# Two of each expert's eight second products in rounded form, and a new order around the last layer's transposes

## What is computed

```python
x = x + xattn_0(layernorm(x), ctx, ...)          # softmax of a normalised similarity
x = x + moe(layernorm(x), ...)                   # 8 experts and a shared one, low-rank side path
x = x + xattn_1(ctx, ctx, masks, layernorm(x))   # masked softmax, scores scaled by the normalised x
x = x + lut_ffn(layernorm(x), lut, gate_idx, up_idx, down_idx)

# moe: top 2 of 8 experts for 1024 tokens, 160 tokens for each expert and choice
h = gelu(einsum('ecd,edf->ecf', buf, w1) + b1[:, None, :])      # 256 -> 1024
y = einsum('ecf,efd->ecd', h, w2) + b2[:, None, :]              # 1024 -> 256
y = y + einsum('ecr,erd->ecd', gelu(einsum('ecd,edr->ecr', buf, wd)), wu)
# lut_ffn: weights are looked up, w = lut[idx], 256 -> 688 -> 256
h = silu(x @ gate.T) * (x @ up.T);  out = h @ down.T
```

## Time and profile before

| | |
|---|---|
| median of 3 runs | 305.8 us (305.75 to 312.18) |
| profiled execution | 306.0 us |
| its span | 304.2 us |
| TensorE busy | 290.8 us, 96% |
| VectorE busy | 240.4 us, 79% |
| ScalarE busy | 155.3 us, 51% |
| POOL busy | 116.5 us, 38% |
| TensorE clock granted | full in all of the span |

### The profile page before, as it was taken

How to read it: one execution, slowest core, us unless ns; L and a number is a source line. 1 busy time by engine, 2 the same in 40 slices (tenths; PEclk the granted TensorE clock), 3 DMA queues, 4 the chain that set the end, 5 groups by cost and what they waited for, 6 DMA issues and landing times.

```text
span 304.2 us, 5858 instructions
## 1 busy us (share of the span) xinstructions
PE 290.8 (96%) x1911; PEld 253.1 (83%) x1911; DVE 240.4 (79%) x638; ACT 155.3 (51%) x369; POOL 116.5 (38%) x143
## 2 busy tenths in 40 slices
PE   7988998998999999999999999999999999989895
PEld 5545686977888998989989898999888899979795
DVE  4888878638989888889888898898985768796632
ACT  2677986225554755546556465555533633535210
POOL 7427410150518165280743806042061224443431
PEclk9999999999999999999999999999999999999999
DMA  7933207540958539195482935647044000010101
GB/s 214 328 139 95 80 0 230 171 138 5 296 163 221 172 79 349 52 253 174 101 286 61 291 134 131 209 78 226 1 43 140 0 1 2 0 37 0 37 0 69
DMA packets 21841, 38.06 MB, mean 125 GB/s; under 512 B 3131, under 2 KB 12411, under 8 KB 21820
## 3 DMA queue, kind: packets, MB, share of 16 engines
q1 hardware_dynamic: 17340, 32.55, 32.5%
q0 software_dynamic: 4480, 5.25, 9.2%
HBM read 31.37 MB, written 6.42 MB: 124 GB/s over the span
## 4 chain that ended last, share of the span: by engine, by line
PE 74%; DVE 12%; ACT 7%; issue 2%; POOL 2%; DMA 1%; SPq 0%; DVEq 0%; ACTq 0%
PE yb L799 27%; PE hb L780 27%; PE yb L814 6%; PE hb L925 4%; PE tb L692 4%; PE yb L940 1%; POOL rstd L454 1%; PE rb L940 1%; DVE xn L1195 1%; PE yb L925 1%; DMA projw<-projw_dram 1%; ACT sm L982 1%; DVE bst L1189 1%; DVE h L1667 1%; DVE x L1338 1%
## 5 line engine op out<-in xcount | busy, mean ns | idle before, releaser
L799 PE MATMUL yb<-raw,h 128*128 128x256 f32 x384 | 96.3, 380 | 0.1
L1095 ACT ACTIVATE h<-hb,b 128x320 f32<-128x320 f32 (+1 forms) x80 | 44.5, 558 | 63.7 <-PE hb L780 59.0
L799 PEld LDWEIGHTS yb<-raw,h 128*128 128x128 f32 x384 | 69.0, 189 | 7.4 <-ACT h L1095 0.5
L780 PE MATMUL hb<-xT_hi,w_hi 128*128 128x320 f32 (+1 forms) x180 | 71.4, 397 | 0.5 <-ACT small L1099 0.5
L780 PE MATMUL hb<-xT_lo,w_hi 128*128 128x320 f32 (+1 forms) x180 | 58.7, 326 | 0.0
L780 PE MATMUL hb<-xT_hi,w_lo 128*128 128x320 f32 (+1 forms) x180 | 58.6, 325 | 0.0
L554 POOL DMA_INDIRECT xacc_dram<-ysb,row_of x16 | 28.5, 1778 | 77.8 <-ACT ysb L962 75.4
L1221 DVE COPY_PREDICATED pick<-bits,pick 128x544 int32<-128x544 uint8 x56 | 43.3, 774 | 0.6
L538 POOL DMA_INDIRECT xg<-xnorm_dram,row_of x24 | 28.7, 1197 | 34.4 <-DVE row_of L1479 17.8
L1580 DVE TENSOR_TENSOR w_lo<-raw,w_hi 128x256 fp32r<-128x256 f32 x84 | 34.7, 415 | 7.4 <-ACT w_hi L962 7.3
L780 PEld LDWEIGHTS hb<-xT_hi,w_hi 128*128 128x128 f32 x180 | 33.9, 188 | 5.1 <-issue 2.2
(11 more groups left out here) (226 smaller groups left out, 512.5 us busy)
## 6 DMA issues: line engine op xcount, KB each, us to landing
raw<-w1pack_dram SPq DMA_DIRECT2D x30, 384.0 KB, 4.9
raw<-w2pack_dram SPq DMA_DIRECT2D x30, 384.0 KB
idx<-idx_dram SPq DMA_DIRECT2D x8, 272.0 KB
x<-x_dram SPq DMA_DIRECT2D x4, 256.0 KB, 4.7
xnorm_dram<-xn SPq DMA_DIRECT2D x2, 512.0 KB, 5.8
xacc_dram<-x SPq DMA_DIRECT2D x2, 512.0 KB, 8.4
x<-xacc_dram SPq DMA_DIRECT2D x4, 256.0 KB, 3.9
out_dram<-x SPq DMA_DIRECT2D x4, 256.0 KB, 2.1
```

What stands on the lines that cost most here:

```text
L780: mm = pe.matmul(hb[s % RING][:, 0:n], w[:, s, k * P:(k + 1) * P], a[:, turn, k, 0:n], start=(i == 0), stop=(i == len(terms) - 1))
L799: mm = pe.matmul(yb[c // 2][:, (c % 2) * D:(c % 2 + 1) * D], h, w, start=(s == 0 and c % 2 == 0), stop=(s == STEPS - 1), skip_group_check= ...
L1095: act.activation(hidden(s - 1, shared, turn), bank[:, 0:n], ACT.Gelu, bias=b1[:, expert, s - 1:s])\
```

## The change

It has three parts. In experts, steps 3 and 5 of the second product are no longer fp32. ScalarE copies w2's eighth and the GELU's rows, 256 columns each, into parts of `h_hi`, VectorE subtracts both into `h_lo`, and TensorE runs three fp32r products of the parts for each of the two blocks: six matmuls for two. The third block stays as it was. `h_hi` and `h_lo` are the last layer's buffers, idle until then. In unit 1 `low_rows` also moves ahead of the first two lookup slots.

In the last layer the transposes of batches 2 and 3 move behind the last gate group of the batch before, and the down product that stood behind the next batch's first group moves ahead of it; `finish` moves from group 3 to group 4, behind the split of the transposes. The last batch's second tile gets a bank of its own (`tb[0]`), and its two tiles are added and sent out one by one.

```diff
+ROUNDED = (3, 5)
...
+            for i in range(2):
+                sp.wait_ge(x4_ok, B + i)
+                sp.dma_start(t["out"][B - 1, i * P:(i + 1) * P, :], x[:, 2 * B - 2 + i, :]).then_inc(out_done, 16)
+            sp.wait_ge(out_done, 16 * B + 16)
...
+            def second_rounded(u, s, loads):
+                i = ROUNDED.index(s)
+                pe.wait_ge(pair_lo_ok, u * 4 + 2 * i - 2)
+                for c in range(2):
+                    rows = slice(c * P, (c + 1) * P)
+                    for j, (h, w) in enumerate(((h_hi, h_hi), (h_lo, h_hi), (h_hi, h_lo))):
+                        mm = pe.matmul(yb[0][:, c * D:(c + 1) * D], h[:, 2 + i, rows], w[:, i, :],
+                                       start=False, stop=False, skip_group_check=True)
+                mm.then_inc(mm2, 1)
...
+                    elif s - LAG in ROUNDED and not shared:
+                        second_rounded(u, s - LAG, loads)
...
+                        apart = b == B - 1 and i == 1
+                        out = tb[0][:, 0:D] if apart else down_banks[b % 2][:, i * D:(i + 1) * D]
...
-                if n >= GLAG:
+                if n == 2 * NG - 1 or n == 3 * NG - 1:
+                    transpose_x3(n // NG + 1)
                     down((n - GLAG) // NG, (n - GLAG) % NG)
-                if n % NG == 4 and n // NG + 1 < B:
-                    transpose_x3(n // NG + 1)
+                    down((n - GLAG + 1) // NG, (n - GLAG + 1) % NG)
+                elif n >= GLAG and n != 2 * NG and n != 3 * NG:
+                    down((n - GLAG) // NG, (n - GLAG) % NG)
+                if n == NG - 2:
+                    transpose_x3(1)
...
+            def pair_weights_hi(u, turn, i):
+                s = ROUNDED[i]
+                act.wait_ge(raw2_in[turn][s // 3], (u - turn) * 8 + 16)
+                act.wait_ge(mm2, u * STEPS - STEPS + s + 1)
+                copy(h_hi[:, i, :], raw2[:, turn, s, :]).then_inc(pair_hi_ok, 1)
+            def pair_rows_hi(u, turn, i):
+                s = ROUNDED[i]
+                act.wait_ge(h32_ok, u * NF + s)
+                copy(h_hi[:, 2 + i, :], hidden(s - 1, False, turn)[:, 0:S]).then_inc(pair_hi_ok, 1)
...
+            def pair_lo(u, turn, i):
+                s = ROUNDED[i]
+                dve.wait_ge(pair_hi_ok, u * 4 + 2 * i - 3)
+                dve.wait_ge(mm2, u * STEPS - STEPS + s + 1)
+                dve.tensor_tensor(h_lo[:, i, :], raw2[:, turn, s, :], h_hi[:, i, :].bitcast(F32), ALU.subtract)\
+                    .then_inc(pair_lo_ok, 1)
+                dve.wait_ge(pair_hi_ok, u * 4 + 2 * i - 2)
+                dve.tensor_tensor(h_lo[:, 2 + i, :], hidden(s - 1, False, turn)[:, 0:S], h_hi[:, 2 + i, :].bitcast(F32),
+                                  ALU.subtract).then_inc(pair_lo_ok, 1)
...
-                    if s == 1 and u:
+                    if s == 1 and u and not after_shared:
                         low_rows(u, UTOK if shared else SLOTS)
...
+                    if s == 0 and after_shared:
+                        low_rows(u, SLOTS)
...
+                if f == 4 and b > 0:
+                    finish(b - 1)
...
-                if f == 3 and b > 0:
-                    finish(b - 1)
-            finish(B - 1)
+            last = 2 * B - 2
+            dve.wait_ge(last_tile_mm, 1)
+            dve.tensor_tensor(x[:, last, :], x[:, last, :], down_banks[(B - 1) % 2][:, 0:D], ALU.add).then_inc(x4_ok, 1)
+            dve.wait_ge(down_mm, B * NG)
+            dve.tensor_tensor(x[:, last + 1, :], x[:, last + 1, :], tb[0][:, 0:D], ALU.add).then_inc(x4_ok, 1)
```

More of the change, by code:

```diff
@@ L289, in program @@
         low_third_ok = sem("low_third_ok")
+        pair_hi_ok = sem("pair_hi_ok")
+        pair_lo_ok = sem("pair_lo_ok")
         up_hi_ok = sem("up_hi_ok")
@@ L307, in program @@
         down_mm = sem("down_mm")
+        last_tile_mm = sem("last_tile_mm")
         x4_ok = sem("x4_ok")
@@ L429, in _ @@
                              t["xacc"][S * b:S * b + S, :].rearrange("(i p) d -> p i d", p=P)).then_inc(x_back[b], 16)
-            for b in range(B):
+            for b in range(B - 1):
                 sp.wait_ge(x4_ok, b + 1)
@@ L433, in _ @@
                     .then_inc(out_done, 16)
-            sp.wait_ge(out_done, 16 * B)
+            for i in range(2):
+                sp.wait_ge(x4_ok, B + i)
+                sp.dma_start(t["out"][B - 1, i * P:(i + 1) * P, :], x[:, 2 * B - 2 + i, :]).then_inc(out_done, 16)
+            sp.wait_ge(out_done, 16 * B + 16)
         @block.gpsimd
@@ L939, in down @@
                         at = DOWN0 + f * D
-                        mm = pe.matmul(down_banks[b % 2][:, i * D:(i + 1) * D], h[0:K, n % GRING, i * P:(i + 1) * P],
-                                       w[0:K, at:at + D], start=(f == 0 and i == 0 and j == 0),
+                        apart = b == B - 1 and i == 1
+                        out = tb[0][:, 0:D] if apart else down_banks[b % 2][:, i * D:(i + 1) * D]
+                        mm = pe.matmul(out, h[0:K, n % GRING, i * P:(i + 1) * P],
+                                       w[0:K, at:at + D], start=(f == 0 and j == 0 and (i == 0 or apart)),
                                        stop=(f == NG - 1 and j == 2), skip_group_check=True)
+                    if b == B - 1 and f == NG - 1 and i == 0:
+                        mm.then_inc(last_tile_mm, 1)
                 mm.then_inc(down_mm, 1)
@@ L1127, in unit @@
                     gelu(u, g, s, shared, turn)
+                    if not shared and s in ROUNDED:
+                        pair_rows_hi(u, turn, ROUNDED.index(s))
                     if u_is(u, 0):
@@ L1138, in unit @@
                         split_hi(g + AHEAD, (s + AHEAD) % STEPS, u + (s + AHEAD) // STEPS)
+                    if not shared and s + 1 in ROUNDED:
+                        pair_weights_hi(u, turn, ROUNDED.index(s + 1))
                     if s == 6 and width:
@@ L1521, in weights_of @@
                 dve.tensor_copy(wsel[:, turn, :], wmap[:, u - 1, :]).then_inc(wsel_ok, 1)
+            def pair_lo(u, turn, i):
[7 more added lines that the diff above has]
+                                  ALU.subtract).then_inc(pair_lo_ok, 1)
             def unit(u, turn, shared=False, after_shared=False, width=0, extra=None):
                 for s in range(STEPS):
-                    if s == 1 and u:
+                    if not shared and s in ROUNDED:
+                        pair_lo(u, turn, ROUNDED.index(s))
+                    if s == 1 and u and not after_shared:
                         low_rows(u, UTOK if shared else SLOTS)
```

## The result

The changed kernel takes 303.25 us (median of 20 runs, 301.95 to 308.6), the one before 305.87 us in the same comparison (20 runs). The ratio is 0.990, with a 95% interval of 0.989 to 0.992: 2.6 us are won by the medians and 3.0 by the ratio, where 4.5 were forecast. The measured time lies inside the range and inside 2%. Some executions of either kernel lie 5 to 6.4 us higher; the comparisons leave them out, and the profiled executions of two experiments (c2_work, b3_one_out) are such, with the third block of expert 1 already 6 us late (94.13 and 93.67 for 88.04 and 87.60), so that only distances behind that place are read from them.

A forecast was written before the change was run, and what follows sets the result against it. TensorE, busy 96% of 304.2 us, was taken to bound the kernel. Terms 2.4 + 0.4 + 1.0 + 0.7 = 4.5 us gave 301.3 us against the median, range 299.8 to 304.0 us.

The forecast's parts named there:

- the last tile: Last output tile: smaller last add and a 128 KB last transfer win 0.7 us, bounds 0.25 to 1.3.
- expert 1: Expert 1: lowrank split ahead of the lookup starts TensorE 1.5 us earlier; 0.4 us kept after a 1.1 us wait.
- two rivals (303.9 and 303.7 us): VectorE's lateness or another chain eats most, chance 0.17; products no faster because of six stationary loads, chance 0.04.
- Rounded products: Experts' steps 3 and 5: six fp32r matmuls take 0.71 us instead of 0.86, saving 2.4 us over sixteen products.
- The pace worked out from the fp32 step: Rounded products at 0.645 us a step, saving 3.4 us in all, 300.3 us; chance 0.10.
- the rival in which the loads eat the gain: Rounded products no faster than before, loading six stationary blocks for four; 303.7 us, chance 0.04.
- The cover of VectorE: Experts: VectorE's added 1.33 us fits, 17.65 us busy of 18.26, covered by about 0.6 us an expert.
- slower than before: Experts: VectorE sets the pace, waiting for copies before steps 3 and 5; 308.0 us, chance 0.05.
- Last layer: Last layer: new order wins 1.0 us behind batch 3's transposes, bounds 0 to 2.9 us.
- the row chain: Last layer: VectorE's and ScalarE's chain to xn gets some 0.15 us later; over 0.2 us longer would refute the prediction.
- I take 0.45 us for it: Last output transfer: halving it to 128 KB saves 0.45 us of 2.1 us to landing, bounds 0 to 1.05.
- The first rival: VectorE's lateness in experts, or another chain, eats most and the last layer wins nothing; 303.9 us, chance 0.17.

The follow-up runs named there:

- c2_work: Kernel before plus the pairs' copies and subtractions on ScalarE and VectorE, TensorE keeping its fp32 products unchanged; ratio 1.0001 (0.999 to 1.001).
- b3_one_out: Follow-up run whose edit and time the text doesn't state; in its profile the read-back landed 4.64 us after an issue at 231.48.
- b1_exps: Changed kernel with unit 9's exponentials of batches 0 and 1 moved from behind step 6 to behind step 7; 302.92 to 303.30 us, ratio 0.991.
- a1_pairs: Kernel before with the rounded second products alone; ratio 0.994 (0.992 to 0.996), profiled execution 304.98 us.
- c4_exps_reads: Changed kernel with unit 9's exponentials behind step 7 and reads of batches 2 and 3 held until batch 0 landed; 302.97 to 303.51 us, ratio 0.991.
- a4_tile: Kernel before with the last output tile apart, nothing else; ratio 1.000 (0.999 to 1.0015).

## Why the prediction was right, and where it was wrong

The time lies in the range and its largest term held. The sum was 1.9 us too large at the median of the runs and 2.2 in the profiled execution, for three reasons: the last tile (0.6 us), expert 1 (0.3) and a late landing that no term had (1.4), less 0.2 us by which the products and the last layer gave more. By the number alone, 303.25 us lies nearer to two rivals (303.9 and 303.7 us) than to the forecast of 301.3; what those rivals described did not happen, save that another chain, in another place, took its share. That the range held in spite of the chain left out is in part its width.

**Rounded products.** Forecast 0.71 us a product, 18.26 us an expert, 2.4 us in all; measured 0.71, 18.26 and, alone, 2.53 us in the experts, of which 0.08 is an earlier start of expert 1 (73.32 for 73.40). The pace worked out from the fp32 step, 0.645 us, is out; so is the rival in which the loads eat the gain. The cover of VectorE held: 17.87 us busy where 17.65 were summed, no wait for h_lo in experts 4 to 8, and the added work alone costs nothing (c2_work). So the rival "slower than before" is out for the place that it named.

**Expert 1.** The mechanism was right: TensorE starts at 72.09 (forecast 71.9) and then waits 0.89 us for h_lo (forecast 1.1). PE's timeline there (to the earlier trace rows):

```profile
72.09 0.48 PE L817 MATMUL yb<-w_up,lowrank 128*128 128x256 f32 x2
...
76.94 0.39 PE L798 MATMUL yb<-h_hi 128*128 128x256 f32 x1 [0.89 <-DVE h_lo L1576]
```

The term, 0.4 us, was mis-sized, by less than the third block's rows say: that of expert 1 starts at 87.73 with the pairs alone and at 87.67 with both, 0.06 us. But the two executions did not enter the expert alike: VectorE's first w_lo of it starts at 70.82 with the pairs alone and at 71.01 with both. In b1_exps, the same code up to there, it starts at 70.79, and PE's timeline has

```profile
76.72 0.39 PE L798 MATMUL yb<-h_hi 128*128 128x256 f32 x1 [0.87 <-DVE h_lo L1576]
```

where a1_pairs has 77.11: 0.39 us, the term as forecast. What the step did not count is the restart. Behind the wait the first two matmuls start 0.23 us apart (76.94, 77.17) and not 0.12, so that 0.28 us are left at the third block (87.45 in b1_exps), 0.03 of them an earlier start; c4_exps_reads shows the same within 0.01 us. No further wait stands in expert 1 or 2 of the changed kernel.

**Last layer.** Forecast 1.0 us, measured 1.05 (1.1 alone), in the way described: a wait of 1.09 us before batch 3's transposes, none before its gate group, the row chain not noticeably longer (transposes 1.12 us earlier, the GELU of unit 9 1.18 us earlier; 0.06 instead of the forecast 0.15).

**Last tile.** Forecast 0.7, measured 0.07 in the profile and nothing in a4_tile. The step that failed is "I take 0.45 us for it", the transfer's share. The add is done 0.27 us sooner after the last matmul, as forecast (0.25). But the second issue ends 0.50 us behind the add (299.11 to 299.61), where the one before took 0.40, and from there to the end of the span it is 2.3 us with 128 KB, 2.2 us with 256 KB before. The lower bound of the transfer's share, all of it fixed, was the true value, and the bound of the whole term, 0.25, was still too high, since the issue behind another one took 0.10 us back. The Trainium skill (DMA: Bandwidth & Descriptors, Anatomy of one DMA) gives, for transfers that GpSimd issues, about 2.0 us of fixed cost, most of it the receipt of the last byte, and bytes over 436 GB/s for the rest, an estimated 0.3 us for the 128 KB saved; these transfers are SyncE's, and the trace, 2.2 and 2.3 us in all, is near the fixed part and shows nothing of the 0.3.

**What was left out.** The sum took for granted that all behind the experts moves forward with TensorE's queue. Unit 9 was not read. It holds a chain, scatter to read-back to statistics to exponentials to GELU, that in the kernel before ended within some 0.3 us of the moment at which TensorE needed it: the product ahead starts at 239.77 and takes 1.73 us (eight records, as elsewhere in the unit), the one behind the GELU starts at 241.76. The view of PE's waits has no row for it, but the chain that ended last of the kernel before passes through this very place:

```profile
239.72 1.28 ACT L1095
...
241.02 0.70 ACT h L1095
...
241.76 1.99 PE yb L799 x8
```

The first rival spoke of "another chain", but placed it in the experts and the last layer. In the upper group of runs the late landing takes 1.4 us off the sum. Terms as they stand in the changed kernel's profiled execution (0.06 for expert 1, with its later start): 2.53 + 0.06 + 1.05 + 0.07 - 1.41 = 2.3 us, the profiled span's 304.2 less 301.9. Without the late landing it would be 3.7 us, about the 3.85 us by which the lower group (302.02) lies under 305.87.

## What to carry to other kernels

Before adding up gains on the engine that is always busy, follow each chain that leaves it and comes back (here through a scatter, a read-back and two other engines) and write down how late it is needed; one that is just in time leaves no row among the waits and takes the next gain away, and only the chain that ended last, read piece by piece, shows it. Of two gains that both bring the same engine forward, ask which queue pays for both: lowrank alone gave 1.4 us, with the pairs 0.3 at most. Splitting a last output transfer is worth only what it saves ahead of the issue, and the extra issue takes a part of that back.

## What the runs showed of the hardware

A read-back of 256 KB, first of four, was seen 2.83 to 2.93 us after its issue in six programs and 3.95 to 4.67 us in five others, in step with where an instruction fetch fell; with two of the four reads held back it was 3.22 and 2.98 us. The cause is not shown, the size is.

Six fp32r matmuls of 256 columns take 0.71 us, 0.118 us each, and the four records of fp32 for the same product 0.86 us, so that the three rounded products cost 0.83 of one fp32 product. Behind a wait (0.28 to 0.89 us) the first of the six and the second start 0.22 to 0.23 us apart, not 0.12.

Between the last exponential and the GELU of unit 9, ScalarE's rows go from 238.53 to 239.84, 1.31 us, of which 1.28 is the load of the table. The Trainium skill (ScalarE: Activation LUTs, What ACT_TABLE_LOAD costs) states about 1.28 us for the load and another 1.38 us of drain, 2.66 us in all for a switch; the trace agrees on the load and leaves no room for a drain behind work that has just ended.
